# Attention output of a transformer block kept transposed: normalised through DRAM by GpSimd instead of by TensorE and VectorE

## What is computed

```
attn = softmax(einsum('bnd,bmd->bnm', q * scale, k) + bias)     # b = 4 images x 12 heads = 48
out  = einsum('bnm,bmd->bnd', attn, v)                          # n = m = 1024, d = 16
out  = out.reshape(b, heads, n, hd).transpose(0, 2, 1, 3).reshape(b, n, 192) @ proj_w.T + proj_b
x    = x + out
t    = x + moe(layernorm(x))
```

## Time and profile before

| | us |
|---|---|
| median of 3 runs (lowest, highest) | 872.07 (870.79, 873.03) |
| the profiled execution | 876.79 |
| its span, first to last instruction | 874.9 |
| TensorE busy in it | 778.5 |
| VectorE busy | 712.4 |
| ScalarE busy | 629.1 |
| GpSimd busy | 288.8 |

### The profile page before, as it was taken

How to read it: one execution, slowest core, us unless ns; L and a number is a source line. 1 busy time by engine, 2 the same in 40 slices (tenths; PEclk the granted TensorE clock), 3 DMA queues, 4 the chain that set the end, 5 groups by cost and what they waited for, 6 DMA issues and landing times. The chain is left out here.

```text
span 874.9 us, 31945 instructions
## 1 busy us (share of the span) xinstructions
PE 778.5 (89%) x11798; PEld 478.8 (55%) x11798; DVE 712.4 (81%) x983; ACT 629.1 (72%) x1142; POOL 288.8 (33%) x437
## 2 busy tenths in 40 slices
PE   4999838999999999999999999999989625999994
PEld 1678803444444444444444444444468615999994
DVE  5976767998999999998999999999527665888883
ACT  3676605888888888888888888888945524666662
POOL 5630000023343433302233233421114403677762
PEclk9999957999999999999999999999989656999998
DMA  6346973445555555445454544554043504555550
GB/s 177 82 135 194 359 227 100 107 121 136 134 145 138 133 132 139 116 119 144 114 135 134 139 143 134 147 146 108 4 163 121 173 27 74 120 128 125 140 109 15
DMA packets 89866, 114.56 MB, mean 131 GB/s; under 512 B 40267, under 2 KB 56809, under 8 KB 88274
## 3 DMA queue, kind: packets, MB, share of 16 engines
q1 hardware_dynamic: 79248, 80.35, 33.9%
q0 software_dynamic: 9248, 26.51, 11.5%
q10 hardware_dynamic: 1314, 6.95, 2.1%
HBM read 77.58 MB, written 33.19 MB: 127 GB/s over the span
## 5 line engine op out<-in xcount | busy, mean ns | idle before, releaser
L913 DVE TENSOR_REDUCE neg_max<-max_ps 128x1 f16<-128x1024 f32 x384 | 451.9, 1221 | 40.6 <-PE max_ps L762 33.2
L896 ACT ACTIVATE probs<-ring_ps 128x512 f32<-128x512 f32 x768 | 413.6, 596 | 67.7 <-PE ring_ps L796 58.8
L796 PE MATMUL ring_ps<-q_side,k_side 113*32 113x512 f16 x3072 | 240.8, 385 | 10.6 <-DMA q_side<-rel_split 7.4
L808 PE MATMUL out_ps<-probs,values 128*32 128x256 f32 x3072 | 200.3, 380 | 0.2 <-ACT probs L896 0.2
L762 PE MATMUL max_ps<-k_side,q_side 48*128 48x256 f16 x1536 | 137.4, 280 | 18.2 <-ACT ident L871 9.3
L808 PEld LDWEIGHTS out_ps<-probs,values 128*32 128x32 f32 x3072 | 92.6, 110 | 70.9 <-issue 1.0
L796 PEld LDWEIGHTS ring_ps<-q_side,k_side 113*32 113x32 f16 x3072 | 73.2, 94 | 95.7 <-ACT probs L896 41.8
L658 POOL COPY max_copies<-neg_max 128x32 f16<-128x32 f16 x48 | 10.1, 210 | 349.4 <-DVE neg_max L913 349.4
L762 PEld LDWEIGHTS max_ps<-k_side,q_side 48*128 48x128 f16 x1536 | 49.3, 95 | 121.8 <-issue 68.9
L1478 PE MATMUL hid_ps<-slot_t,w_top 128*118 128x128 f16 x312 | 69.0, 221 | 0.3 <-DMA slot_t<-slot_rows 0.3
L1479 PE MATMUL hid_ps<-slot_t,w_top 128*118 128x128 f16 x312 | 68.8, 221 | 0.0
(11 more groups left out here) (231 smaller groups left out, 1319.6 us busy)
## 6 DMA issues: line engine op xcount, KB each, us to landing
q_side<-rel_split SPq DMA_DIRECT2D x384, 64.0 KB, 2.3
q_side<-qk_split SPq DMA_DIRECT2D x192, 64.0 KB, 2.4
rel_split<-expert_weights ACTq DMA_DIRECT2D x6, 1024.0 KB, 4.9
rel_split<-expert_weights SPq DMA_DIRECT2D x6, 1024.0 KB, 6.0
q_side<-qk_split SPq DMA_DIRECT2D x48, 128.0 KB, 2.7
k_side<-qk_split SPq DMA_DIRECT2D x144, 32.0 KB, 1.8
token_rows<-tn_parts SPq DMA_DIRECT2D x8, 512.0 KB, 3.4
expert_weights<-in_w_t POOLq DMA_DIRECT2D x32, 117.2 KB, 3.0
```

The lines of the kernel that those rows point to most:

```text
L796: last = nc.tensor.matmul(ring_ps[turn_of(k) % BANKS][at:at + COLS, :], k_side[slot(s)][:, tile * P + at:tile * P + at + COLS], queries, s ...
L808: last = nc.tensor.matmul(out_ps[quarter * 2 * HD:(quarter + 1) * 2 * HD, :], values[j][:, tile, :], probs[:, u % 2 * GROUP + 2 * i + quar ...
L896: nc.scalar.activation(probs[:, u % 2 * GROUP + i, :], ring_ps[turn_of(k) % BANKS][:], ACT.Exp).then_inc(exp_done, 1)
L913: nc.vector.tensor_reduce(neg_max[:, j % 2, t:t + 1], max_ps[t % 2][:], AX, ALU.max, negate=True).then_inc(tile_max, 1)
```

## The change

The attention output is no longer turned back. The values get sixteen columns of ones in place of one (rows 16 to 31 of each block all hold the sums), and ScalarE copies `out_ps` to one of four buffers `out_t`. For head n, in later steps, all on GpSimd's queue unless said:

1. step n+1: the four rows of sums go to DRAM (`store_sums`), and at that step's end come back as 128x8 (`load_sums`);
2. step n+2: VectorE takes the reciprocal of 128x8 (`invert_sums`), it goes to DRAM (`store_inverse`), and at that step's end is read into `spread`, each quarter's row on 32 partitions (`spread_inverse`);
3. step n+3: GpSimd multiplies 128x256 (`scale_output`) and stores the result to `att_dram` (`store_output`).

SyncE's queue reads `att_dram` back into `att_t`, channels on the partitions, in steps 28 to 31 and 47 (`load_outputs`); the last head of each image goes straight from SBUF to SBUF (`place_output`). The `gate` stage projects from `att_t` without turning or copying, and finishes the last three heads itself. The load of the third expert matrix (`load_experts`) moves behind the last head's placement. SyncE's loop over heads is written out. Some buffers now share memory (the tokens' transposes with `out_t` and `spread`, the output matrix's split with `att_t`).

```diff
@@ new functions
+def store_sums(queue, g, n):
+    queue.wait_ge(g.out_copied, n + 1)
+    queue.dma_start(g.sums_dram[n % 2], g.out_t[HD::2 * HD, n % OUTS, :]).then_inc(g.sums_stored[n % 2], 16)
+def load_sums(queue, g, n):
+    queue.wait_ge(g.sums_stored[n % 2], 16 * (n // 2 + 1))
+    queue.dma_start(g.sums[:, n % 2, :], g.sums_dram[n % 2].rearrange("q n -> (q n)").rearrange("(p c) -> p c", p=P)).then_inc(g.sums_loaded[n % 2], 16)
+def invert_sums(nc, dve, g, slot, head, reused):
+    dve.wait_ge(g.sums_loaded[slot % 2], 16 * (B // 2 * head + slot // 2 + 1))
...
+    nc.vector.reciprocal(g.inverse[:, slot % 2, :], g.sums[:, slot % 2, :]).then_inc(g.inverted, 1)
+def store_inverse(queue, g, n):
+    queue.wait_ge(g.inverted, n + 1)
+    queue.dma_start(g.inverse_dram[n % 2]..., g.inverse[:, n % 2, :]).then_inc(g.inverse_stored[n % 2], 16)
+def spread_inverse(queue, g, n):
+    queue.wait_ge(g.inverse_stored[n % 2], 16 * (n // 2 + 1))
...
+    queue.dma_start(g.spread[:, n % 2, :], every_row).then_inc(g.inverse_spread[n % 2], 16)
+def scale_output(nc, pool, g, n):
+    pool.wait_ge(g.inverse_spread[n % 2], 16 * (n // 2 + 1))
...
+    nc.gpsimd.tensor_tensor(g.scaled[:, n % 2, :], g.out_t[:, n % OUTS, :], g.spread[:, n % 2, :], ALU.mult).then_inc(g.output_scaled, 1)
+def store_output(queue, g, n):
+    queue.wait_ge(g.output_scaled, n + 1)
...
+    queue.dma_start(by_quarter, g.scaled[:, n % 2, :]).then_inc(g.placed[image], 16)
+def place_output(sp, g, n):
...
+        sp.dma_start(g.att_t[C - HD:C, 1, queries], g.scaled[...]).then_inc(g.last_placed[image], 16)
@@ attention, GpSimd, step n
+                if s.before(3):
+                    scale_output(nc, pool, g, s.n - 3)
+                if s.before(1):
+                    store_sums(pool, g, s.n - 1)
+                if s.before(2):
+                    store_inverse(pool, g, s.n - 2)
+                if 3 <= s.n < BH - 1:
+                    store_output(pool, g, s.n - 3)
...
+                if n >= 1:
+                    load_sums(pool, g, n - 1)
+                if n >= 2:
+                    spread_inverse(pool, g, n - 2)
@@ attention, TensorE
-                    if u == 2 and s.before(1):
-                        bank_free(s, TURNED_AT)
-                        turn_out(s.n - 1)
@@ attention, ScalarE
-                if reused:
-                    act.wait_ge(turned, n)
-                nc.scalar.activation(out_t[:], out_ps[:], ACT.Copy).then_inc(out_copied, 1)
+                if reused:
+                    act.wait_ge(g.output_scaled, n - 3)
+                nc.scalar.activation(g.out_t[:, j, :], out_ps[:], ACT.Copy).then_inc(g.out_copied, 1)
@@ attention, VectorE
-                    if u == 2 and s.before(1):
-                        normalize(s.n - 1, head(s, -1), slot(s, -1), s.before(2))
+                    if u == 1 and s.before(2):
+                        invert_sums(nc, dve, g, slot(s, -2), head(s, -2), s.before(4))
@@ gate, TensorE
             def project_out(s):
-                pe.wait_ge(at_ready, 2 * s + 2)
+                if s % 2 == 0:
+                    pe.wait_ge(g.outputs_loaded[s // 2], 32)
+                    pe.wait_ge(g.last_placed[s // 2], 64)
...
-                if b + 1 < STEPS:
-                    turn_attention(b + 1)
```

More of the change, by code:

```diff
@@ new lines, in store_output @@
+def store_output(queue, g, n):
+    queue.wait_ge(g.output_scaled, n + 1)
+    head, image = n // B, n % B
+    by_quarter = g.att_dram[head, :, image * N:(image + 1) * N].rearrange("c (q n) -> q c n", q=4)
+    queue.dma_start(by_quarter, g.scaled[:, n % 2, :]).then_inc(g.placed[image], 16)
+def place_output(sp, g, n):
+    sp.wait_ge(g.output_scaled, n + 1)
+    image = n % B
+    for q in range(4):
+        queries = slice(image * N + q * N // 4, image * N + (q + 1) * N // 4)
+        sp.dma_start(g.att_t[C - HD:C, 1, queries], g.scaled[2 * HD * q:2 * HD * q + HD, n % 2, :]).then_inc(g.last_placed[image], 16)
@@ L545, with load_outputs @@
+HALF_HEADS = HEADS // 2
+def load_outputs(sp, g, image, c):
+    heads = range(HALF_HEADS) if c == 0 else range(HALF_HEADS, HEADS - 1)
+    tokens = slice(image * N, (image + 1) * N)
+    sp.wait_ge(g.placed[image], 16 * heads.stop)
+    sp.dma_start(g.att_t[0:HD * len(heads), c, tokens], g.att_dram[heads.start:heads.stop, 0:HD, tokens]).then_inc(g.outputs_loaded[image], 16)
+OUTS = 4
 K_LO = HD + 2 * HS
@@ L618, in _ @@
         def _(sp):
+            TOPS_LOADED = B * HALF_HEADS + 4
             def store_max(n, j):
@@ L641, in step @@
                     load_positions(sp, g, head(s, 3), slot(s, 3))
-            steps(sp, BH, SLOTS, step)
+                if TOPS_LOADED <= s.n < TOPS_LOADED + B:
+                    load_outputs(sp, g, s.n - TOPS_LOADED, 0)
+                if s.n == BH - 1:
+                    for image in range(B):
+                        load_outputs(sp, g, image, 1)
+                    place_output(sp, g, BH - 4)
+            for n in range(BH):
+                step(Step(n, n // SLOTS, n % SLOTS, BH, True))
         @block.gpsimd
@@ L777, in bank_free @@
                         return pe.wait_ge(max_copied, s.n - back + 2)
[L778 to L781 removed]
+                    if at not in (MAX_AT, UNUSED_AT):
+                        k = at - (at > MAX_AT)
                         return pe.wait_ge(exp_done, 2 * KT * (s.n - back) + k + 1)
@@ L1012, in _ @@
         def _(sp):
-            load_experts(sp, g, experts_loaded)
+            last = BH - 1
+            place_output(sp, g, last - 2)
+            place_output(sp, g, last - 1)
             def store_residual(s):
@@ L1027, in _ @@
                     store_residual(b)
+                if b == 2:
+                    place_output(sp, g, last)
+                    load_experts(sp, g, experts_loaded)
                 if b >= LAG + 1:
@@ L1061, in _ @@
                     normalize(b - 2)
+                if b == 2:
+                    scale_output(nc, pool, g, last)
         @block.tensor
```

155 lines of the change are left out of this document (71 added, 84 removed).

## The result

The changed kernel takes 984.62 us (median of four runs, 978.02 to 988.63), the kernel before 872.55 in the same comparison: a ratio of 1.126, interval 1.122 to 1.130. The forecast was 852, its range 838 to 868. It missed by 133 us and on the wrong side.

The account below looks back on a forecast made before the run. VectorE was taken to bound the attention, with TensorE adding a little. Attention -16.2, late splitting steps +4, attention's end -1.2 and gate stage -7 gave -20.4 us: 852 us against 872.07, range 838 to 868.

Parts of the forecast that it names:

- VectorE in the attention, 10.15 us a head: Attention: VectorE's 9.74 us of work plus 0.41 of waits, 0.36 less than 10.51 a head, 16.2 us in 45 heads.
- What costs nothing ... Traffic grows by some 256 KB a head on engines that are half busy: DMA: the added transfers, some 256 KB a head on engines busy 0.52, were costed at nothing.
- GpSimd, "4.7 of the 7.0 us are gone, and an ordinary step is hidden": Attention: GpSimd's added work and wait fit its idle time, except in eight splitting steps at 0.5 us each, +4 us.
- the sums land too late: Rival, attention: VectorE's reciprocal waits for late sums and stops the reductions behind it; up to 894 us, chance 0.09.
- The reductions wait for nothing of it: Attention: VectorE's new reciprocal, 0.20 us a head, would not make its reductions wait.
- Reciprocals wait for GpSimd: Rival, attention: each VectorE reciprocal stands behind a GpSimd product of 0.55 us, +25 us, 877 us; chance 0.07.
- The gate stage waits for the last head: Rival, gate stage: with landings of 4.1 us the stage gains nothing, 860 us; chance 0.06.
- The pace is held by TensorE's list: Rival, attention: TensorE's waits grow by what VectorE saves, so the attention gains nothing, 864 us; chance 0.15.
- End of the attention, -1.2: Between the last output copy and the gate stage: turning and normalising fall away, about 1.2 us less.
- The gate stage, -7, first residual 2.5 to 3 us after its start: Gate stage: projection starts at once, first residual 4.5 us sooner, turns saved; -7 us, between -10 and +1.
- The sum: Whole kernel: the forecast's terms together, -16.2 + 4 - 1.2 - 7 = -20.4 us.

Follow-up runs that it names:

- thirteenth: Changed kernel with four loads of positions ahead of the row of maxima and a whole head between each sums-chain transfer and its user: 904.83 us, 1.038.
- seventh experiment: Kernel before, plus two unneeded transfers a head of 128 KB in 1 KB pieces on GpSimd's queue: 920.96 us, 1.054.
- eighth: Kernel before, plus four unneeded transfers a head of 4 KB in 32-byte pieces on GpSimd's queue: 892.98 us, 1.020.
- twelfth: Kernel before, with four loads of positions ahead of the row of maxima and two unneeded 128 KB transfers a head on GpSimd's queue: 874.62 us, 1.002.
- fourteenth: Changed kernel with a whole head between each sums-chain transfer and its user, all eight loads of positions behind the row of maxima: 972.49 us, 1.115.
- first experiment: Changed kernel with GpSimd's product of head n-3 and the store of its result moved to the end of its step: 943.83 us, 1.082.
- second: Changed kernel with the product multiplying the output by itself, so not waiting for the spread, which is still transferred: 976.15 us (one run).
- ninth experiment: Kernel before, with four of the eight loads of positions ahead of the store of the row of maxima on SyncE: 869.73 us, 0.9942.
- fourth experiment: Changed kernel with the attention's last load of sums and last spread issued first in the gate stage: 979.59 and 975.25 us in two runs.
- fifth: Changed kernel with four of the eight loads of positions ahead of the store of the row of maxima on SyncE: 977.00 us, 1.114.

## Why the prediction was wrong

*VectorE in the attention, 10.15 us a head: near in the pace where nothing waits, and wrong in the gain.* The undisturbed heads of the changed kernel and of its repairs take 10.0 to 10.25 us (10.19 in the median of the thirteenth), and the reciprocal took 0.19 us. But the median head of the kernel before takes 10.34 us, not 10.51: my 10.51 was a mean that already held the heads in which TensorE waited for positions. The gain is 0.15 us a head, some 7 us in 45 heads and not 16.2. That the pace came out near is luck: it started too high and took off too much.

*"What costs nothing ... Traffic grows by some 256 KB a head on engines that are half busy": this step failed, and it is the largest.* I read a share of busy time (0.52) and not the waits that end on a transfer. The kernel before has one, 5.6 us over nine times between 200 and 600 us, and no term of mine rests on it. On the kernel before, the seventh experiment prices such traffic at 46 us and the eighth small pieces by themselves at 18; the twelfth shows the mechanism (with room for the positions the same transfers cost 5 to 7 us), and in the changed kernel the room for positions is worth 68 us (fourteenth against thirteenth). The Trainium skill (DMA: Bandwidth & Descriptors, Issuing engines are not separate DMA queues) says that transfers of SyncE and of GpSimd run on the same 16 DMA engines and interleave. The seventh experiment agrees: traffic on GpSimd's queue made the median landing of positions on SyncE's 2.8 us instead of 2.3.

*GpSimd, "4.7 of the 7.0 us are gone, and an ordinary step is hidden": failed.* The sum counted product, issues and the wait for the reciprocal, but not the product's wait for the spread that was issued at the end of the step before. It came to 112.1 us between 200 and 600 us. The product was mis-sized as well (0.73 us for 0.55), and so were the five issues (0.56 to 0.72 us each, 3.17 together, for 2.66). Opening this loop gave 41 us in the first experiment; when I removed the same wait together with the need for the spread (second), it gave 8. Which place in a head the transfers then fall on may matter: TensorE's wait for positions was 22.9 us between 200 and 700 us in the first and 52.2 in the second. Why is not settled.

*The rival "the sums land too late": the right kind of wait, at a smaller share.* It priced landings of 4.8 to 5.7 us, and 4.9 is what they took; VectorE's wait was 23.3 us in 400. The reductions do stand behind it, so "The reductions wait for nothing of it" was wrong too. I had given it 0.09 for a landing of 2.2 us, from a row of another size at another time. The Trainium skill (DMA: Bandwidth & Descriptors, Anatomy of one DMA) gives 2.0 us plus the bytes at 436 GB/s for a transfer of GpSimd's queue, as an estimate 2.0 us for 4 KB and 2.3 for 128 KB; the trace differs, with 4.9 and 5.7 us between other transfers, and it decides.

*The other rivals.* "Reciprocals wait for GpSimd" is refuted by the 0.19 us (0.204 at most in 48). "The gate stage waits for the last head" did not happen: TensorE waited for no placement there, though the stage also began late. "The pace is held by TensorE's list" came true in part. Stretch and VectorE's wait from 160 to 200 us, where heads are undisturbed, first in the thirteenth and then in the ninth experiment:

```profile
160.00:200.00 40.00, 39.44 (x640) 17.37 (x632) 37.60 (x35) 36.03 (x72) 14.76 (x27) 1.00 0.51 134
DVE neg_max L1010 <- PE max_ps L874: 2.5, 8, 0.3
```

```profile
160.00:200.00 40.00, 39.72 (x700) 18.50 (x692) 37.98 (x38) 35.38 (x71) 7.31 (x15) 1.00 0.45 122
DVE neg_max L914 <- PE max_ps L763: 1.2, 5, 0.3
```

VectorE has less to do without the normalisation, and waits longer for raw scores. The 9.29 us that I set against this rival come from heads in which TensorE computes no raw scores either (27.1 us of its time between 250 and 350 us), so they do not bound a head with them.

*End of the attention, -1.2: failed.* From the end of the last copy to the gate stage's start were 1.46 us and are 8.73. The changed kernel's timeline there:

```profile
746.94 0.38 ACT L973 ACTIVATE out_t<-out_ps 128x256 f32<-128x256 f32 x1 [1.19 <-PE out_ps L911]
...
748.86 0.71 POOL L577 DMA_DIRECT2D spread<-inverse_dram  x1 [0.24 <-DMA inverse_dram<-inverse]
...
749.90 0.17 POOL L851 MEMSET expert_weights<- 128x48 f16 x1
...
756.49 0.57 POOL L545 DMA_DIRECT2D sums_dram<-out_t  x1 [6.42 <-POOLq L647]
...
759.28 0.56 DVE L1258 TENSOR_TENSOR x_sb<-proj_ps,x_sb 128x384 f32<-128x384 f32 x1 [1.32 <-PE proj_ps L1164]
```

GpSimd's last spread was issued at 748.86 and landed 3.3 us later, and behind GpSimd's clearing at 749.90 no engine went on before 756. The fourth experiment bears out that GpSimd's last transfers hold part of this; what holds the 3.9 us behind that landing stays open.

*The gate stage, -7, first residual 2.5 to 3 us after its start: the mechanism right, the size too large.* It comes 3.2 us after ScalarE's start there (756.05). From the stage's start to the end of the span are 226.9 us (982.9 - 756.05), and 231.3 before (874.9 - 643.62): 4.4 less, inside the bounds, for the 7 forecast.

*The sum.* Not -20.4, but of span -0.6 ahead of the attention, +105.8 in it, +7.3 at its end and -4.4 behind it.

## What to carry to other kernels

Before adding transfers to a kernel, list every wait in it that ends on a DMA, however small, and follow each round its loop: copy, issues in the queue, landing, the engine's wait. Here one that was closed to a few tenths of a microsecond made added traffic cost 18 and 46 us, and moving four issues into the queue's own idle time brought the 46 down to 5. Where several loops hold the pace, opening one can show almost nothing (8 us in the second and fifth experiments); test them together before calling either innocent. And give a wait for a fresh transfer a landing at its worst in traffic, not the best row of the profile: an engine that works in order passes the wait on to all that is queued behind it.

## What was not expected of the hardware

- A load of 4 KB in pieces of 32 bytes took as long to land (4.9 us) as larger ones (4.6 for a store of 128 KB, 5.7 for the spread), and 16 KB a head in such pieces slowed the kernel before by 18 us.
- Medians of landings hid what mattered. The positions' median went from 2.3 to 2.4 us, and TensorE's wait for them from 5.6 to 32.5 us: a head waits for the last of its loads, and the one behind the wait of 3.00 us landed after 6.8.
- After a wait of 3 us TensorE resumed at 0.87, went to 0.50 for 2 us and was at 0.77 in the next 2, so such a wait is paid for again behind it.
- A row of 8 KB landed after 9.2 us with a load of 384 KB issued 2.6 us behind it.
